# Attention's sums of exponentials: the two key halves added on POOL, one product with ones per head instead of two

## The chip, the cores and the metric

The kernel runs on one core of one Trainium2 chip. The metric is the device time of one execution, in microseconds (us). Engines are named as the profile names them: PE (matrix products), PEld (its weight loads), DVE (VectorE), ACT (ScalarE), POOL (GpSimd) and SP (the queue that issues transfers).

## What is computed

A decoder layer on 16 batches of 256 rows and 512 channels, in float32: self-attention with 16 heads of 32 channels (each of its four linear maps has a low-rank addition), then a decayed scan over a second input, then a feed-forward block with ternary weights and inner size 2048. Each of the three ends in a residual sum and a layer norm. The part that the change touches is the softmax of the attention:

```python
q = _split(lora_linear(x, Wq, bq, Bq, Aq))
k = _split(lora_linear(x, Wk, bk, Bk, Ak))
v = _split(lora_linear(x, Wv, bv, Bv, Av))
scores = jnp.einsum('bhqd,bhkd->bhqk', q, k) * SCALE
attn = jax.nn.softmax(scores, axis=-1)
out = jnp.einsum('bhqk,bhkd->bhqd', attn, v)
...
h = jax.nn.silu(bitlinear158(x, w1, b1))
h = jax.nn.gelu(h, approximate=False)
h = layer_norm(h, ln_g, ln_b)
return bitlinear158(h, w2, b2)
```

## The kernel before, in words

**Work and order.** Every engine has a hand-written program: a loop over j from 0 to 18 whose body works on several batches at once. Batch j is in its attention, batch j-1 in the scan and the first feed-forward product, batch j-2 in the feed-forward layer norm, batch j-3 in the last product. The order within a body is written out by hand on each engine, and every engine works its list in order. Semaphores tie the lists together: `wait(engine, name, b, k)` waits until step k of batch b was counted under that name. For j from 2 to 15 all the attention and all or nearly all of the rest is present; j of 0 and 1 also prepare the weights of the feed-forward block, and j from 16 to 18 have no attention.

**Attention.** The 16 heads are done in four groups of four, c = 0 to 3. The 256 keys are two halves of 128, which lie on the partitions. For each group PE computes the scores with queries on the partitions (`scores`, L1079), and DVE takes the row maxima from them (`maxima`, L769). PE transposes the maxima (`shiftT`, L1088), and ACT stores them (L554). PE then computes the scores again with keys on the partitions and the maxima subtracted (`shifted`, L1103), and ACT takes the exponentials (`probs_of`, L532, two instructions, one per key half) into `probs` (128 partitions; key half x head x 256 queries). PE multiplies them by the values (`weighted`, L1115) and by ones (L1119). The second product sums the exponentials over the keys: per head it is one product per key half, the two accumulated in PSUM, each with 32 columns of ones, so that the sum comes out on the head's 32 partitions of bank 4. `pv_ready` is counted behind the last of them. DVE turns the sums into their inverse and scales the result (`attn_norm`: L785, L787, L789, L794), and POOL splits it into a high and a low part (`attn_split`: L351, L354), which the output product `o` multiplies.

**PE's body**, in order: y(0) (L1189), o(0) (L1056), qk of group 2, scores 1, weighted 0, o(1), shiftT 1, hT(2) and hT(3) (L1182), shifted 1, qk 3, scores 2, weighted 1, y(1), shiftT 2, r(0) and r(1) (L1156), shifted 2, qk 0 of the next batch, scores 3, weighted 2, v(0), shiftT 3, v(1), shifted 3, qk 1 and scores 0 of the next batch, weighted 3, hT(0) and hT(1), xq(0) and xq(1) (L1164, L1165), eight products f (L1172, L1173) with shiftT 0 of the next batch between them, shifted 0 of the next batch. So between the exponentials of a group and its `weighted` stands one `qk` and one `scores`. y, o, r, v, hT, xq and f share PSUM banks 6 and 7, and each waits for the reader of the bank's last content: r(1) for the DVE sum behind y(1) (L917), xq(1) for `hqT_move` (DVE, L910).

**ACT's body** begins with the exponentials of group 0, then `h_var` (L603), `h_norm` (L608). It ends with `silu` of the eight f and two `gelu` (L593).

**POOL's body**: res1 (L406), two `neg_mean` (L433), inverse_std3 (L394 to L399), h_rstd(0) (L440 to L446, which waits for ACT's `h_var`), g_mul(0) (L452), attn_split 0, h_rstd(1), inverse_std1 (L361 to L367), x_lo of the next batch (L343), attn_split 1, g_mul(1), inverse_std3, inverse_std2 (L376 to L386), x_rms (L421 to L428), z_rms, attn_split 2, res2 (L413), z_rms, attn_split 3.

**DVE's body** holds, among others: L917 and L818 (residual sums with L810 and L812), maxima 1, attn_norm 0, z_add(0) (L873, behind g_mul(0)), maxima 2, attn_norm 1, z_max(0) (L878), L917 of y(1), two sums L826 behind r, z_add(1) (L873), maxima 3, attn_norm 2, quantise_x (L847 to L867; waits for ACT's second norm L570, which waits for POOL's inverse_std2), quantise_z(0) (L896 to L903; hT(0) waits for it), maxima 0 of the next batch, hqT_move (L910), attn_norm 3.

Of the kernel before, what the change touches and what calls it, by code (L numbers as in the profile page):

```python
# [7 lines left out]
F32 = mybir.dt.float32  # L8
# [5 lines left out]
ALU = mybir.AluOpType  # L14
AX_X = mybir.AxisListType.X

P = 128
NB = 16
T = 256
NT = T // P  # L20
# [3 lines left out]
HD = D // HEADS  # L24
GH = P // HD
# [25 lines left out]
def decoder_kernel(nc, x, xT, ctxT, W, L, bq, bk, bv, bo, decay, w1T, b1, ln_g, ln_b, w2T, b2, out):  # L51
    b1_scratch = nc.dram_tensor("b1_scratch", (NPART, INNER), BF16, kind="Internal").ap()

    with ExitStack() as ctx:
        def sb(name, shape, dt):
            return ctx.enter_context(nc.sbuf_tensor(name, shape, dt))
# [34 lines left out]
        inverse_T = sb("inverse_T", [P, T // HD], F32)  # L91
        inverse = sb("inverse", [P, T], F32)
        probs = sb("probs", [P, NT, GH, T], F32)
        attn = sb("attn", [P, T], F32)
        attn_hi = sb("attn_hi", [P, KC, T], F32R)
        attn_lo = sb("attn_lo", [P, KC, T], F32R)
# [26 lines left out]
        def sem(name):  # L123
# [44 lines left out]
            (DV, "z_added", 4), (DV, "z_quant", 12),  # L168
            (DV, "ln3", 6), (DV, "hqT_moved", 1),

            (PO, "x_lo", 1), (PO, "attn_split", 8), (PO, "res1", 2), (PO, "res2", 2), (PO, "rstd1", 3),
            (PO, "rstd2", 4), (PO, "rstd3", 6), (PO, "x_rms", 4), (PO, "h_stat", 8), (PO, "g_mul", 2),
            (PO, "z_rms", 4),

# [5 lines left out]
        def wait(eng, name, b, k):  # L180

            if b * per[name] + k > 0:
                eng.wait_ge(S[name], b * per[name] + k)

        def alive(j, lag):

            return 0 <= j - lag < NB
# [34 lines left out]
        def flat(t):  # L222
            return t.rearrange("p a b -> p (a b)")
# [100 lines left out]
        def _(po):  # L324
# [13 lines left out]
            def x_lo(b):  # L338
# [4 lines left out]
                po.tensor_tensor(flat(xT_lo[:, :, :]), flat(xT_in[:, :, :]), flat(xT_hi[:, :, :].bitcast(F32)),  # L343
                                 ALU.subtract).then_inc(S["x_lo"], 1)

            def attn_split(b, c):

                wait(po, "attn_done", b, c + 1)
                if c == 0:
                    wait(po, "o_ready", b - 1, 2)  # L350
                po.tensor_scalar(attn_hi[:, c, :], attn[:, :], 1.0, 0.0, ALU.mult,  # L351
                                 ALU.add).then_inc(S["attn_split"], 1)
                wait(po, "attn_split", b, 2 * c + 1)
                po.tensor_tensor(attn_lo[:, c, :], attn[:, :], attn_hi[:, c, :].bitcast(F32),  # L354
                                 ALU.subtract).then_inc(S["attn_split"], 1)

            def inverse_std1(b):

                r = rstd[:, 0, :, :]
                wait(po, "ln1", b, 6)  # L360
                po.tensor_scalar(r[:, R_VE, :], mean_var[:, 0, :, 1], 1.0, EPS, ALU.mult,  # L361
                                 ALU.add).then_inc(S["rstd1"], 1)
                wait(po, "rstd1", b, 1)
                po.tensor_tensor(r[:, R_USED, :], r[:, R_VE, :], neg_half[:, :], ALU.pow).then_inc(S["rstd1"], 1)
                wait(po, "rstd1", b, 2)
                for q in range(NT):
                    last = po.tensor_scalar(r[:, R_NB, q:q + 1], mean_var[:, 0, q, 0:1], r[:, R_USED, q:q + 1],  # L367
                                            -1.0, ALU.mult, ALU.mult)
                last.then_inc(S["rstd1"], 1)
# [39 lines left out]
            def res2(b):  # L409

                for q in range(NT):
                    wait(po, "x_quant", b, 6 + q)
                    po.tensor_tensor(rows_of(b)[:, q, :], rows_of(b)[:, q, :], b2_tile[:, :],  # L413
                                     ALU.add).then_inc(S["res2"], 1)
# [21 lines left out]
            def h_rstd(b, q):  # L436

                f = fs[:, q, :]
                wait(po, "h_var", b, q + 1)
                po.tensor_scalar(f[:, H_VE:H_VE + 1], f[:, H_VS:H_VS + 1], 1.0 / INNER, EPS, ALU.mult,  # L440
                                 ALU.add).then_inc(S["h_stat"], 1)
                wait(po, "h_stat", b, 3 + 3 * q)
                po.tensor_tensor(f[:, H_RSTD:H_RSTD + 1], f[:, H_VE:H_VE + 1], neg_half[:, 0:1],
                                 ALU.pow).then_inc(S["h_stat"], 1)
                wait(po, "h_stat", b, 4 + 3 * q)
                po.tensor_tensor(f[:, H_NB:H_NB + 1], f[:, H_NMEAN:H_NMEAN + 1], f[:, H_RSTD:H_RSTD + 1],  # L446
                                 ALU.mult).then_inc(S["h_stat"], 1)

            def g_mul(b, q):

                wait(po, "h_normed", b, q + 1)
                po.tensor_tensor(h_of(b, q)[:, :], h_of(b, q)[:, :], g_tile[:, :], ALU.mult).then_inc(S["g_mul"], 1)  # L452
# [22 lines left out]
            def body(j):  # L475
                if alive(j, 1):
                    res1(j - 1)
                if alive(j, 2):
                    neg_mean(j - 2, 0)
                    neg_mean(j - 2, 1)  # L480
                if alive(j, 3):
                    inverse_std3(j - 3, 0)
                if alive(j, 2):
                    h_rstd(j - 2, 0)
                    g_mul(j - 2, 0)
                if alive(j, 0):
                    attn_split(j, 0)
                if alive(j, 2):
                    h_rstd(j - 2, 1)
                if alive(j, 1):  # L490
                    inverse_std1(j - 1)
                if alive(j, -1):
                    x_lo(j + 1)
                if alive(j, 0):
                    attn_split(j, 1)
                if alive(j, 2):
                    g_mul(j - 2, 1)
                if alive(j, 3):
                    inverse_std3(j - 3, 1)
                if alive(j, 1):  # L500
                    inverse_std2(j - 1)
                    x_rms(j - 1)
                if alive(j, 2):
                    z_rms(j - 2, 0)
                if alive(j, 0):
                    attn_split(j, 2)
                if alive(j, 1):
                    res2(j - 1)
                if alive(j, 2):
                    z_rms(j - 2, 1)  # L510
                if alive(j, 0):
                    attn_split(j, 3)
# [522 lines left out]
        def _(pe):  # L1035
# [71 lines left out]
            def weighted(b, c):  # L1107

                wait(pe, "attn_done", b, c)
                wait(pe, "v_stored", b, 2)  # L1110
                wait(pe, "probs_ready", b, 2 * (c + 1))
                for kt in range(NT):
                    for i in range(GH):
                        ch = (GH * c + i) * HD
                        pe.matmul(bank[4][i * HD:(i + 1) * HD, 0:T], v_sb[b % 2][:, kt, ch:ch + HD], probs[:, kt, i, :],  # L1115
                                  start=(kt == 0), stop=(kt == NT - 1))
                for kt in range(NT):
                    for i in range(GH):
                        last = pe.matmul(bank[4][i * HD:(i + 1) * HD, T:2 * T], ones[:, :], probs[:, kt, i, :],  # L1119
                                         start=(kt == 0), stop=(kt == NT - 1))  # L1120
                last.then_inc(S["pv_ready"], 1)


# [221 lines left out]
```

## Time and profile before

| | |
|---|---|
| time of three executions | 1217.88, 1218.5, 1220.4 us; median 1218.5 us |
| profiled execution | time 1219.12 us, span 1216.9 us |
| busy share of the span | PE 88%, PEld 59%, DVE 70%, ACT 68%, POOL 48% |
| mean granted TensorE clock | 0.953 of full speed |
| transfers | 51.79 MB, 43 GB/s on average |

The span is the stretch from the first to the last instruction of the profiled execution; its own time is 2.2 us longer. A busy share is the time in which the engine ran at least one instruction. PE's instructions overlap, and in the rows of the trace an f32 product has two records: a group of eight is `x16`.

### The profile page before, as it was taken

What the parts mean: (1) busy time and instruction counts of PE and PEld (TensorE: products, weight loads), DVE (VectorE), ACT (ScalarE), POOL (GpSimd) and SP (SyncE); (2) the same over time, 40 slices, a digit from 0 to 9 for tenths busy, and PEclk for the clock granted to TensorE, in tenths of its full rate; (3) what the DMA queues carried; (4) which work ended last, traced back from release to release, by engine and by line L of the source; (5) the groups of instructions that cost most, each with busy time, mean ns of one, the idle gap of its engine ahead of it and who ended that gap; (6) DMA issues with size and microseconds to landing.
All of it is one profiled execution on the core that took longest, in us unless ns stands there. A gap on an engine that the chain in (4) does not pass through costs nothing.

```text
span 1216.9 us, 25870 instructions
## 1 busy us (share of the span) xinstructions
PE 1065.3 (88%) x10572; PEld 714.9 (59%) x10572; DVE 851.3 (70%) x1358; ACT 828.5 (68%) x1019; POOL 583.9 (48%) x767
## 2 busy tenths in 40 slices
PE   4977888999999999999999999999999999967253
PEld 3666647575666667575756666675757566643121
DVE  4366938687695968686876959686868769585524
ACT  3555576776778677867767786778677677866472
POOL 2203318273654637282736546372827365463433
PEclk8999889999999999999999999999999999989587
DMA  7522101001010201001010102010010101010000
GB/s 287 190 73 85 53 1 53 1 28 44 13 60 2 71 1 39 33 27 44 28 44 12 60 2 71 2 44 27 28 44 28 44 13 42 1 53 1 18 6 29
DMA packets 17783, 51.79 MB, mean 43 GB/s; under 512 B 2809, under 2 KB 2809, under 8 KB 15874
## 3 DMA queue, kind: packets, MB, share of 16 engines
q1 hardware_dynamic: 16946, 48.31, 11.4%
q8 instruction: 84, 1.38, 0.5%
q10 hardware_dynamic: 720, 1.84, 0.4%
q14 instruction: 33, 0.27, 0.1%
HBM read 41.73 MB, written 8.40 MB: 41 GB/s over the span
## 4 chain that ended last, share of the span: by engine, by line
PE 71%; DVE 11%; ACT 7%; issue 5%; POOL 4%; DMA 1%; SPq 0%; ACTq 0%; POOLq 0%; DVEq 0%
PE bank L1056 29%; PE bank L1172 11%; PE wave L1103 9%; PE bank L1189 5%; PE wave L1079 4%; PE bank L1115 4%; PE bank L1173 3%; PE bank L1119 3%; DVE shift L769 3%; DVE fz L878 2%; POOL h L452 2%; PE bank L1182 2%; ACT hqT L626 2%; ACT h L608 1%; DVE qk_parts L778 1%
## 5 line engine op out<-in xcount | busy, mean ns | idle before, releaser
L769 DVE TENSOR_REDUCE shift<-wave 128x8 f32<-128x2048 f32 x64 | 146.8, 2294 | 102.1 <-PE wave L1079 102.1
L532 ACT ACTIVATE probs<-wave 128x1024 f32<-128x1024 f32 x128 | 124.4, 1024 | 108.9 <-PE wave L1103 108.8
L452 POOL TENSOR_TENSOR h<-h,g_tile 128x2048 f32<-128x2048 f32 x32 | 146.3, 4571 | 42.7 <-ACT h L608 41.2
L1172 PE MATMUL bank<-w,xqT 128*128 128x512 fp8e4 x512 | 135.9, 389 | 12.9 <-ACT invT L579 7.8
L1189 PE MATMUL bank<-w,hqT 128*128 128x512 fp8e4 x512 | 121.0, 391 | 17.3 <-ACT hqT L626 16.4
L587 ACT ACTIVATE h<-bank,qx 128x512 f32<-128x512 f32 x128 | 88.0, 688 | 62.3 <-PE bank L1173 61.0
L433 POOL TENSOR_SCALAR fs<-fs 128x1 f32<-128x1 f32 x32 | 6.2, 192 | 221.1 <-ACT h L593 221.1
L917 DVE SCALAR_TENSOR_TENSOR rows<-bank,fz,rows 128x512 f32<-128x512 f32 x32 | 23.9, 747 | 113.4 <-PE bank L1189 113.4
L1103 PE MATMUL wave<-qk_parts 32*128 32x256 f32 x1536 | 92.0, 337 | 11.2 <-ACT shift_rows L554 11.2
L873 DVE TENSOR_TENSOR h<-h,b_tile 128x2048 f32<-128x2048 f32 x32 | 75.5, 2360 | 36.9 <-POOL h L452 36.9
L1189 PEld LDWEIGHTS bank<-w,hqT 128*128 128x128 bf16 x512 | 48.7, 100 | 84.8 <-ACT hqT L626 18.0
L570 ACT ACTIVATE rows<-rows,rstd 128x512 f32<-128x512 f32 x96 | 74.7, 817 | 31.2 <-POOL rstd L399 11.4
L1056 PE MATMUL bank<-xT_hi,wq_hi 128*128 128x256 f32 x256 | 78.8, 308 | 8.3 <-DVE wk_lo L762 7.2
L1103 PE MATMUL wave<-shift_rows,ones_wide 32*128 32x256 f32 x1024 | 85.6, 397 | 0.0
L1172 PEld LDWEIGHTS bank<-w,xqT 128*128 128x128 bf16 x512 | 41.5, 98 | 70.6 <-issue 22.0
L547 ACT ACTIVATE qk_parts<-bank,bias_qk 128x256 fp32r<-128x256 f32 x128 | 54.0, 479 | 40.5 <-PE bank L1056 40.5
L1103 PEld LDWEIGHTS wave<-qk_parts 32*128 32x128 f32 x1536 | 66.0, 192 | 24.9 <-ACT shift_rows L554 13.7
L351 POOL TENSOR_SCALAR attn_hi<-attn 128x256 fp32r<-128x256 f32 x64 | 26.2, 410 | 109.8 <-DVE attn L794 98.2
L354 POOL TENSOR_TENSOR attn_lo<-attn,attn_hi 128x256 fp32r<-128x256 f32 x64 | 73.8, 1153 | 5.3
L608 ACT ACTIVATE h<-h,fs 128x2048 f32<-128x2048 f32 x32 | 67.4, 2105 | 13.1 <-POOL fs L446 13.1
L1056 PE MATMUL bank<-xT_lo,wq_hi 128*128 128x256 f32 x256 | 73.1, 286 | 0.0
L1056 PE MATMUL bank<-xT_hi,wq_lo 128*128 128x256 f32 x256 | 72.9, 285 | 0.0
(155 smaller groups left out, 3008.2 us busy)
## 6 DMA issues: line engine op xcount, KB each, us to landing
ctx_sb<-ctxT SPq DMA_DIRECT2D x16, 512.0 KB, 3.6
rows<-x SPq DMA_DIRECT2D x16, 512.0 KB, 3.9
out<-rows SPq DMA_DIRECT2D x32, 256.0 KB, 2.1
xT_in<-xT SPq DMA_DIRECT2D x15, 512.0 KB, 5.0
h<-w1T SPq DMA_DIRECT2D x4, 1024.0 KB, 4.9
h<-w2T SPq DMA_DIRECT2D x4, 1024.0 KB, 5.8
h<-Wq SPq DMA_DIRECT2D x1, 1024.0 KB, 6.1
h<-Wk SPq DMA_DIRECT2D x1, 1024.0 KB, 10.2
```

Of the source, the lines that this page charges most:

```text
L354: po.tensor_tensor(attn_lo[:, c, :], attn[:, :], attn_hi[:, c, :].bitcast(F32), ALU.subtract).then_inc(S["attn_split"], 1)
L452: po.tensor_tensor(h_of(b, q)[:, :], h_of(b, q)[:, :], g_tile[:, :], ALU.mult).then_inc(S["g_mul"], 1)
L532: ac.activation(probs[:, kt, :, :], wave[:, :, kt * T:(kt + 1) * T], ACT.Exp, scale=SM_SCALE).then_inc(S["probs_ready"], 1)
L570: ac.activation(rows_of(b)[:, q, :], rows_of(b)[:, q, :], ACT.Identity, scale=r[:, R_USED, :], bias=r[:, R_NB, :]).then_inc(S[f"norm{ln}"], 1)
L587: ac.activation(h_of(b, q)[:, n * FW:(n + 1) * FW], bank_of("f", u), ACT.Silu, scale=qx[:, X_DEQ, q:q + 1]).then_inc(S["silu_done"], 1)
L608: ac.activation(h_of(b, q)[:, :], h_of(b, q)[:, :], ACT.Identity, scale=fs[:, q, H_RSTD:H_RSTD + 1], bias=fs[:, q, H_NB:H_NB + 1]).then_in ...
L769: dv.tensor_reduce(shift[:, :, :, 0].rearrange("p t j -> p j t"), wave[:, :, :].rearrange("p j (t k) -> p j t k", t=NT), axis=AX_X, op=ALU ...
L873: dv.tensor_tensor(h_of(b, q)[:, :], h_of(b, q)[:, :], b_tile[:, :], ALU.add).then_inc(S["z_added"], 1)
L1056: last = pe.matmul(psum, lhsT, rhs, start=(i == 0), stop=(i == len(pairs) - 1))
L1103: last = pe.matmul(bank[head][:, kt * T:(kt + 1) * T], keys, queries, start=(i == 0), stop=(i == 3))
L1172: pe.matmul(p[:, :], xqT[:, q, kc, :], w1[:, kc, n * FW:(n + 1) * FW], start=(kc == 0), stop=False)
L1189: last = pe.matmul(p[:, :], hqT[:, k, :], w2[:, k, :], start=(k == 0), stop=(k == FC - 1))
```

## The change

POOL gets a step `add_halves` for each group: it waits for both key halves' exponentials and for the products of the group before, and adds the two halves of `probs` (128 x 1024 each) into a tile of its own, `half_sum`, of which there is one. In `weighted` PE multiplies that tile by ones, one product per head in place of two. It waits for POOL behind the eight products with the values. In POOL's body the step of group 0 stands between h_rstd(0) and g_mul(0), that of group 1 between inverse_std1 and x_lo, that of group 2 between the second inverse_std3 and inverse_std2, and that of group 3 between res2 and the last z_rms.

```diff
@@ tiles and counts
+        half_sum = sb("half_sum", [P, GH, T], F32)
...
+            (PO, "halves_added", 4),
@@ POOL
+            def add_halves(b, c):
+
+                wait(po, "probs_ready", b, 2 * (c + 1))
+                wait(po, "pv_ready", b, c)
+                po.tensor_tensor(flat(half_sum[:, :, :]), flat(probs[:, 0, :, :]), flat(probs[:, 1, :, :]),
+                                 ALU.add).then_inc(S["halves_added"], 1)
@@ POOL, body(j)
                 if alive(j, 2):
                     h_rstd(j - 2, 0)
+                if alive(j, 0):
+                    add_halves(j, 0)
+                if alive(j, 2):
                     g_mul(j - 2, 0)
...
                 if alive(j, 1):
                     inverse_std1(j - 1)
+                if alive(j, 0):
+                    add_halves(j, 1)
                 if alive(j, -1):
                     x_lo(j + 1)
...
                 if alive(j, 3):
                     inverse_std3(j - 3, 1)
+                if alive(j, 0):
+                    add_halves(j, 2)
                 if alive(j, 1):
                     inverse_std2(j - 1)
                     x_rms(j - 1)
...
                 if alive(j, 1):
                     res2(j - 1)
+                if alive(j, 0):
+                    add_halves(j, 3)
                 if alive(j, 2):
                     z_rms(j - 2, 1)
@@ PE, weighted(b, c)
-                for kt in range(NT):
-                    for i in range(GH):
-                        last = pe.matmul(bank[4][i * HD:(i + 1) * HD, T:2 * T], ones[:, :], probs[:, kt, i, :],
-                                         start=(kt == 0), stop=(kt == NT - 1))
+                wait(pe, "halves_added", b, c + 1)
+                for i in range(GH):
+                    last = pe.matmul(bank[4][i * HD:(i + 1) * HD, T:2 * T], ones[:, :], half_sum[:, i, :],
+                                     start=True, stop=True)
                 last.then_inc(S["pv_ready"], 1)
```

The order of POOL's instructions from h_rstd(0) of one body to x_lo, in the kernel before (`fs` holds the feed-forward statistics, `h` its rows):

```order
L440 TENSOR_SCALAR fs<-fs 128x1 [waits h_var]
L443 TENSOR_TENSOR fs<-fs,neg_half 128x1 [waits h_stat]
L446 TENSOR_TENSOR fs<-fs 128x1 [waits h_stat]
L452 TENSOR_TENSOR h<-h,g_tile 128x2048 [waits h_normed]
L351 TENSOR_SCALAR attn_hi<-attn 128x256 [waits o_ready,attn_done]
L354 TENSOR_TENSOR attn_lo<-attn,attn_hi 128x256 [waits attn_split]
...
L367 TENSOR_SCALAR rstd<-mean_var,rstd 128x1 [waits rstd1]
L367 TENSOR_SCALAR rstd<-mean_var,rstd 128x1
L343 TENSOR_TENSOR xT_lo<-xT_in,xT_hi 128x1024 [waits v_ready,qk_ready,x_hi]
```

And the same stretch in the changed kernel, whose lines stand eight further down the file:

```order
L448 TENSOR_SCALAR fs<-fs 128x1 [waits h_var]
L451 TENSOR_TENSOR fs<-fs,neg_half 128x1 [waits h_stat]
L454 TENSOR_TENSOR fs<-fs 128x1 [waits h_stat]
L351 TENSOR_TENSOR half_sum<-probs 128x1024 [waits pv_ready,probs_ready]
L460 TENSOR_TENSOR h<-h,g_tile 128x2048 [waits h_normed]
L359 TENSOR_SCALAR attn_hi<-attn 128x256 [waits o_ready,attn_done]
L362 TENSOR_TENSOR attn_lo<-attn,attn_hi 128x256 [waits attn_split]
...
L375 TENSOR_SCALAR rstd<-mean_var,rstd 128x1 [waits rstd1]
L375 TENSOR_SCALAR rstd<-mean_var,rstd 128x1
L351 TENSOR_TENSOR half_sum<-probs 128x1024 [waits pv_ready,probs_ready]
L344 TENSOR_TENSOR xT_lo<-xT_in,xT_hi 128x1024 [waits v_ready,qk_ready,x_hi]
```

The sum of group 0 now stands behind h_rstd(0) and its wait for ACT, and ahead of g_mul(0); that of group 1 stands behind g_mul(0) and everything up to inverse_std1, ahead of x_lo.

PE's `weighted` of a group in the changed kernel (`bank` is bank 4), where eight products `bank<-probs,ones` without a wait of their own stood before:

```order
L1132 MATMUL bank<-probs,v_sb 32x256 [waits probs_ready,v_stored]
L1132 MATMUL bank<-probs,v_sb 32x256 x7
L1136 MATMUL bank<-half_sum,ones 32x256 [waits halves_added]
L1136 MATMUL bank<-half_sum,ones 32x256 x3
```

Four products are gone, and the first of the remaining four waits for POOL.

## Rows read from the trace of the kernel before

**Rows 1.** The page's chain that ended last: shares of the span by engine.
```profile
PE 71%; DVE 11%; ACT 7%; issue 5%; POOL 4%; DMA 1%; SPq 0%; ACTq 0%; POOLq 0%; DVEq 0%
```
**Rows 2.** Windows: one body: length; busy us (count) of PE, PEld, DVE, ACT, POOL; PEclk; DMA.
```profile
503.80:570.70 66.90, 63.92 (x659) 43.47 (x658) 50.59 (x82) 49.37 (x63) 35.44 (x47) 1.00 0.11 33
```
**Rows 3.** Groups by line and form: line, engine, tiles, shapes, count | busy, mean ns | idle before.
```profile
L1119 PE MATMUL bank<-probs,ones 128*32 128x256 f32 x1024 | 68.2, 384 | 0.0
...
L343 POOL TENSOR_TENSOR xT_lo<-xT_in,xT_hi 128x1024 fp32r<-128x1024 f32 x16 | 37.9, 2369 | 18.2 <-ACT xT_hi L540 18.2
...
L452 POOL TENSOR_TENSOR h<-h,g_tile 128x2048 f32<-128x2048 f32 x32 | 146.3, 4571 | 42.7 <-ACT h L608 41.2
...
L361 POOL TENSOR_SCALAR rstd<-mean_var 128x2 f32<-128x2 f32 x16 | 3.1, 193 | 1.6 <-DVE mean_var L812 0.4
...
L859 DVE TENSOR_SCALAR qx<-qx,w_mean 128x2 f32<-128x2 f32 x16 | 19.9, 1246 | 0.0
```
**Rows 4.** PE in order of time, that body: start, length, instruction [idle before it].
```profile
514.78 1.05 PE L1119 MATMUL bank<-probs,ones 128*32 128x256 f32 x16
...
526.67 1.05 PE L1119 MATMUL bank<-probs,ones 128*32 128x256 f32 x16
...
533.42 0.66 PE L1156 MATMUL bank<-ident,ctx_sb 128*128 128x128 f32 x4 [1.49 <-DVE rows L917]
...
540.60 1.05 PE L1119 MATMUL bank<-probs,ones 128*32 128x256 f32 x16
...
554.12 1.05 PE L1119 MATMUL bank<-probs,ones 128*32 128x256 f32 x16
555.10 1.07 PE L1182 MATMUL bank<-ident_bf,h 128*128 128x128 bf16 x16
...
557.47 0.40 PE L1164 MATMUL bank<-ident_bf,x_round 128*128 128x128 bf16 x4
```
**Rows 5.** ACT in order of time, the same body.
```profile
513.28 0.20 ACT L603 ACTIVATION_READ_ACCUMULATOR junk<-h,fs 128x1 f32 x1
...
535.93 1.94 ACT L532 ACTIVATE probs<-wave 128x1024 f32<-128x1024 f32 x2 [3.32 <-PE wave L1103]
...
541.78 1.53 ACT L570 ACTIVATE rows<-rows,rstd 128x512 f32<-128x512 f32 x2
...
549.44 1.94 ACT L532 ACTIVATE probs<-wave 128x1024 f32<-128x1024 f32 x2 [0.46 <-PE wave L1103]
```
**Rows 6.** POOL in order of time, the same body.
```profile
514.46 0.19 POOL L446 TENSOR_TENSOR fs<-fs 128x1 f32<-128x1 f32 x1
...
521.91 2.66 POOL L354 TENSOR_TENSOR attn_lo<-attn,attn_hi 128x256 fp32r<-128x256 f32 x1
...
526.92 0.51 POOL L367 TENSOR_SCALAR rstd<-mean_var,rstd 128x1 f32<-128x1 f32 x2
...
537.48 2.15 POOL L376 TENSOR_SCALAR rstd<-mean_var 128x2 f32<-128x2 f32 x1 [0.47 <-DVE mean_var L812]
```
**Rows 7.** DVE in order of time, the same body.
```profile
521.50 2.48 DVE L873 TENSOR_TENSOR h<-h,b_tile 128x2048 f32<-128x2048 f32 x1 [1.00 <-POOL h L452]
...
528.11 0.44 DVE L785 STREAM_TRANSPOSE sums_T<-bank 128x256 f32<-128x256 f32 x1
...
532.62 0.74 DVE L917 SCALAR_TENSOR_TENSOR rows<-bank,fz,rows 128x512 f32<-128x512 f32 x1
...
537.31 2.26 DVE L873 TENSOR_TENSOR h<-h,b_tile 128x2048 f32<-128x2048 f32 x1
...
544.36 1.21 DVE L847 TENSOR_REDUCE qx<-rows 128x2 f32<-128x1024 f32 x1
...
551.12 0.16 DVE L899 TENSOR_TENSOR fz<-fz 128x1 f32<-128x1 f32 x1
...
551.56 1.29 DVE L903 TENSOR_SCALAR h<-h,fz 128x2048 f32<-128x2048 f32 x1
...
556.27 0.69 DVE L910 TENSOR_SCALAR hqT<-bank 128x1024 bf16<-128x1024 int16 x1 [0.63 <-PE bank L1182]
```

More of the change, by code:

```diff
@@ L169, in decoder_kernel @@
             (DV, "ln3", 6), (DV, "hqT_moved", 1),
-            (PO, "x_lo", 1), (PO, "attn_split", 8), (PO, "res1", 2), (PO, "res2", 2), (PO, "rstd1", 3),
+            (PO, "x_lo", 1), (PO, "halves_added", 4), (PO, "attn_split", 8), (PO, "res1", 2), (PO, "res2", 2), (PO, "rstd1", 3),
             (PO, "rstd2", 4), (PO, "rstd3", 6), (PO, "x_rms", 4), (PO, "h_stat", 8), (PO, "g_mul", 2),
```

## The prediction

> **What bounds the kernel now.** I read the chain of waits first: 71% of the span is PE's work [rows 1]. Then one body in the middle, j = 7: of 66.9 us PE is busy 63.9 at the full granted clock, POOL 35.4 [rows 2]. The bodies of j = 2 to 14 repeat this to about 0.1 us, so I walk through one, at the absolute times of the trace, and multiply. The longest idle time of PE in it is the 1.49 us ahead of r(1), where it waits for DVE's L917 [rows 4]. PE has next to no slack: a microsecond saved counts nearly in full, and so does one of new waiting.
>
> **What PE saves.** The products with ones of a group take 0.98 us from the first to the instruction behind them (554.12 to 555.10) [rows 4], and this holds for each of the 64 groups, whose 1024 records are one group of lines [rows 3]. Half of the products gone is 0.49 us a group, if half the work takes half the time: 1.96 us a body.
>
> **What the add costs POOL.** The trace has no such add. The nearest rows are x_lo, same engine, type of operation and element count, 2.37 us, and half of g_mul, 4.57/2 = 2.29 us [rows 3]. I take 2.3 us. POOL goes from 35.4 to 44.6 us a body: not the bound. What matters is when each add ends and when PE wants it. I reckon 0.6 us from the add's end to the next work of PE (0.05 for the wait, then four products alone: 1.05 - 0.49 us, the group's length less half of its stretch) [rows 4].
>
> **Group 0: a wait of 2.2 us.** PE wants the sum at 514.78 [rows 4]. The add stands behind h_rstd(0). That waits for ACT's h_var, which ends at 513.48 [rows 5], and L446 ends at 514.65 [rows 6]. The add runs from 514.7 to 517.0. PE's next work starts at 517.6 instead of 515.76: **+1.85 us**, the saved half counted. The path to 514.65 runs over f, silu, gelu, the exponentials and h_var, and nothing in it becomes shorter. g_mul(0) starts 0.1 us later.
>
> **Group 1: little more.** POOL then does g_mul(0) to 521.6 and attn_split. z_add(0) on DVE (L873) begins where the split's second half does. Before, L354 took 2.66 us and ended 0.6 us behind L873 [rows 6, 7]; L376, of the form for which L361 takes 0.19 us, took 2.15 us beside the other L873 and ended with it [rows 3, 6, 7]. So an L873 (both inputs in SBUF) stops POOL for its own 2.3 us. Now the split gets in first, z_add runs 522.8 to 525.1, and it is h_rstd(1) that is stopped. inverse_std1 ends at 527.85 (before 527.43) [rows 6], and the add runs 527.9 to 530.2. PE wants it at 526.67 + 1.85 = 528.5: it waits 1.7 us. The sums are ready at 530.8, and attn_norm starts then instead of at 528.11 [rows 7]: DVE is 2.7 us late, with it L917, and with that r(1) on PE. PE, 3.1 us late, gives up most of its old wait there [rows 4]. Both stand at **+2.7 us**. If POOL escaped the stop, DVE would be late by its maxima alone, +1.85.
>
> **Group 2: stopped by z_add(1).** Both chains start at L917: exponentials that ended at 537.87 [rows 5], z_add(1) at 537.31 to 539.57 [rows 7]. z_add is 0.56 us ahead and stays so. At +2.7 it runs 540.0 to 542.3. The add is free to start at 540.6. No row shows two large operations meeting here; between no wait at all and a wait to the end of z_add I take the latter, as L376 showed it. The add runs 542.3 to 544.6, PE wants it at 543.3, and goes on at 545.2 instead of 541.58: **+3.6 us** (without the stop +2.7 - 0.49 = +2.2). The Trainium skill, SBUF — State Buffer, "Who interferes with whom", says that a VectorE instruction with two SBUF inputs and a GpSimd instruction that reads SBUF exclude each other, and that the one issued first keeps the port pair for its whole length. By that rule the group gives +3.6; if the two shared the port it would give +2.2. The small operations of the trace agree with the rule; whether a large add does is not shown.
>
> **Behind group 2.** inverse_std2 now stands behind that add. ACT's second norm began 2.15 us behind L376's end [rows 5, 6]. With the 2.3 us of the tiny operations and nothing to hide them it begins at about 547.05 (+5.3), and quantise_x on DVE at 548.65, not 544.36 (+4.3) [rows 7]. L899 is then due at 555.4. **Group 3's** exponentials end at 551.38 + 3.6 = 555.0 [rows 5], and POOL, long through with res2, adds from 555.0 to 557.3. PE wants it at 557.7: no wait, -0.49. But L899 has two SBUF inputs. L859, a tiny operation beside POOL's res2, takes 1.25 us where L899 takes 0.16 [rows 3, 7]: POOL stops DVE too. So L899 waits to 557.3, L903 ends at 559.1, and hT(0), due on PE at 555.10 + 3.1 = 558.2, starts at 559.15. The next maxima follow, then hqT_move at 561.5 (before 556.27) [rows 7], and xq(1), which needs its bank, starts at 562.25 instead of 557.47 [rows 4]. Through ACT's silu the products f end up at about **+4.5 us**. Without this last effect: +3.1.
>
> **Moved steps and other queues.** x_lo now ends at 532.5; qk of the next batch, which reads it, stands behind shifted 2 and begins at 538.5, so it is hidden. g_mul(1) ends at 538.3, before z_add(1) is due at 540.0: 1.7 us in hand. res2 and attn_split 3 have more. Were that cover gone, each microsecond would go into z_add(1), and so into the add of group 2. SP's and ACT's lists issue no transfer more or later than their bodies. The new wait on PE holds up the output products or y behind it, which is what the sums above count. One `half_sum` tile does no harm: the wait for the group before is long met.
>
> **The sum.** Thirteen bodies (2 to 14) at +4.5 = +58.5 us. Body 15 lacks the next batch's work, and has the same order on POOL: about +4. Bodies 0 and 1 have an idle POOL and can only gain, between 0 and 8 x 0.49 = 3.9 us: -2. The tail has no attention: 0. Together +60.5 us. The profiled execution goes from a span of 1216.9 to 1277.4 us, with the 2.2 us around it 1279.6. Its own time before, 1219.12, is 0.6 above the median of the three executions, 1218.5, so the median becomes **1279 us**, 5.0% more.
>
> **The rivals.**
> 1. *The stops are smaller* (chance 0.28). Group 0's wait stays, since it hangs on ACT alone, but the port costs less, or quantise_z slips in ahead of the add. With the stop of group 2 and no later effect a body loses 1.85 + 0.85 + 0.9 - 0.49 = 3.1 us; with group 0's alone, and groups 2 and 3 saving 0.49 each, 0.9 us (group 1's saving is lost, as r(1) waits for DVE). Times 14, less the 2 us of bodies 0 and 1: 1229 to 1260. For it: the margins in group 3 are 0.4 us. Against: both L354 and L376 are stopped in full.
> 2. *The adds are hidden* (0.05), the other side. The mechanism is PE's saving with the add of group 0 early enough. It decides at 514.78: POOL would have to start by 512.4, 2.3 us earlier than L446's end lets it. Then three groups save 0.49 us and group 1's is lost, 1.47 x 14 + 2 = 23 us: 1196. For it: exponentials of groups 1 to 3 end 2.7 us before the sums are wanted. Against: the order of POOL's list.
> 3. *Four products take as long as eight* (0.08). They lie on four column groups and overlap; if the four that are left cost the 0.98 us of the eight, the saving of 1.96 us a body is none: 14 x 1.96 = 27 us more, 1306. Against: the 16 records of a group are evenly spread over the 0.98 us.
>
> **How the numbers follow.** The forecast has 0.57, the three rivals 0.28, 0.05 and 0.08, and 0.02 is left for no change. A measurement of this kernel can tell about 0.2%, 2.4 us, from no change. Faster by more than that: 0.05; within it: 0.03; slower: 0.92, from the forecast, rivals 1 and 3 and a small rest. The forecast's own range is 1260 to 1292, from the bounds of the last effect (1.4 us a body) and of the add (2.29 to 2.37 us). With most of rival 1 below and part of rival 3 above, the range is 1238 to 1296.
>
> **What would show it right or wrong.** In the changed profile: POOL's add x64 at about 2.3 us, those of group 2 longer, about 4 us, with the stop in them. PE idle ahead of the products with ones, released by POOL: 2.2 us a body in group 0, about 1.7 in group 1, about 1.3 in group 2, none in group 3. The products with ones half as long in all. A body of 71.4 us in place of 66.9. Second norm and quantise_x late, L899 waiting beside the add. Wrong would be: no wait in group 0; an add that isn't stopped beside L873; a body shorter than 67 us.

## The result, and the profile after

The changed kernel takes 1330.22 us (median of four executions, 1324.56 to 1335.95), against 1218.46 us before. The ratio is 1.091, 95% interval 1.086 to 1.097. It is slower, as forecast, but by 112 us and not by 60, and the time lies 34 us above the range. The profiled execution took 1324.56 us, with a span of 1321.4 us.

The page of the changed kernel: busy time by engine, granted PE clock in 40 slices, and the chain that ended last.

```profile
PE 1091.7 (83%) x10060; PEld 698.2 (53%) x10060; DVE 897.3 (68%) x1358; ACT 827.6 (63%) x1019; POOL 732.9 (55%) x831
...
PEclk9998799999999999989989898999989898977677
...
PE 26%; POOL 25%; DVE 19%; ACT 17%; issue 11%; DMA 1%; SPq 0%; POOLq 0%; ACTq 0%; DVEq 0%
```

PE's share of the chain was 71% [rows 1]; now POOL has a quarter, and DVE and ACT have more than before. PE is busy *longer* than before, 1091.7 against 1065.3 us, with 512 records fewer. That is the surprise of this page, and the clock row is the hint: it has 8s in the second half, where the row of the kernel before has 9s.

Two bodies of the changed kernel, windows with the columns of [rows 2]. They start at the first y of the body:

```profile
457.80:529.20 71.40, 62.91 (x627) 42.05 (x627) 53.43 (x82) 49.35 (x63) 44.94 (x51) 1.00 0.09 31
529.20:604.40 75.20, 67.08 (x628) 42.80 (x628) 53.42 (x82) 49.39 (x63) 44.94 (x51) 0.93 0.09 29
```

Both issue the same work, and DVE, ACT and POOL are busy alike. The first is 71.4 us long, as predicted. In the second PE's granted clock averages 0.93, PE is busy 4.2 us longer, and the body is 3.8 us longer. The bodies of j = 3 to 6 are of the first kind, 71.37 or 71.38 us each, those of j = 7 to 14 of the second, 75.1 to 75.2.

PE in order of time in the body of j = 7. The numbers answer to [rows 4]:

```profile
542.39 0.64 PE L1136 MATMUL bank<-half_sum,ones 128*32 128x256 f32 x8 [2.04 <-POOL half_sum L351]
...
555.23 0.64 PE L1136 MATMUL bank<-half_sum,ones 128*32 128x256 f32 x8 [1.18 <-POOL half_sum L351]
...
561.25 0.66 PE L1173 MATMUL bank<-ident,ctx_sb 128*128 128x128 f32 x4 [1.17 <-DVE rows L934]
...
569.68 0.64 PE L1136 MATMUL bank<-half_sum,ones 128*32 128x256 f32 x8 [1.06 <-POOL half_sum L351]
...
582.70 0.61 PE L1136 MATMUL bank<-half_sum,ones 128*32 128x256 f32 x8
...
584.84 1.05 PE L1199 MATMUL bank<-ident_bf,h 128*128 128x128 bf16 x16 [1.52 <-DVE h L920]
586.71 0.61 PE L1181 MATMUL bank<-ident_bf,x_round 128*128 128x128 bf16 x4 [0.82 <-ACT hqT L643]
...
588.53 1.87 PE L1189 MATMUL bank<-w,xqT 128*128 128x512 fp8e4 x4 [0.18 <-ACT invT L596]
```

The waits for POOL are where they were forecast: 2.04, 1.18 and 1.06 us in groups 0 to 2, none in group 3. So is the wait of hT(0) for DVE, 1.52 us (the walk had 0.95). The last row is the one that was not forecast. Each of the eight products f is four matrix products of 128x512 on L1189 and one on L1190; the four of the first f take 1.87 us. The same place in the body of j = 4:

```profile
370.70 1.05 PE L1199 MATMUL bank<-ident_bf,h 128*128 128x128 bf16 x16 [1.52 <-DVE h L920]
372.58 0.40 PE L1181 MATMUL bank<-ident_bf,x_round 128*128 128x128 bf16 x4 [0.82 <-ACT hqT L643]
...
374.14 1.02 PE L1189 MATMUL bank<-w,xqT 128*128 128x512 fp8e4 x4 [0.18 <-ACT invT L596]
```

There the lead-up is the same, the same 1.52 and 0.82 us of waits, but the clock holds. In the body of j = 7 the transposes behind the second wait already take 0.61 us instead of 0.40: the clock falls ahead of the products f.

POOL, ACT and DVE of the body of j = 7, with the stops:

```profile
548.17 2.11 POOL L448 TENSOR_SCALAR fs<-fs 128x1 f32<-128x1 f32 x1
...
552.81 2.37 POOL L351 TENSOR_TENSOR half_sum<-probs 128x1024 f32<-128x1024 f32 x1
...
565.79 3.84 POOL L351 TENSOR_TENSOR half_sum<-probs 128x1024 f32<-128x1024 f32 x1 [1.13 <-ACT probs L549]
...
580.13 2.39 POOL L351 TENSOR_TENSOR half_sum<-probs 128x1024 f32<-128x1024 f32 x1 [0.76 <-ACT probs L549]
```
```profile
572.05 1.52 ACT L587 ACTIVATE rows<-rows,rstd 128x512 f32<-128x512 f32 x2 [2.58 <-POOL rstd L394]
```
```profile
565.14 2.26 DVE L890 TENSOR_TENSOR h<-h,b_tile 128x2048 f32<-128x2048 f32 x1
...
573.61 1.22 DVE L864 TENSOR_REDUCE qx<-rows 128x2 f32<-128x1024 f32 x1 [0.81 <-ACT rows L587]
...
580.25 2.29 DVE L913 TENSOR_TENSOR fz<-fz 128x1 f32<-128x1 f32 x1
```

h_rstd(1)'s first operation is stopped for 1.9 us by z_add(0), which runs from 547.6 to 550.2; the add of group 2 takes 3.84 us, since z_add(1) (L890) has the port until 567.4; the second norm and quantise_x are late; and a 128x1 operation of quantise_z takes 2.29 us beside the add of group 3 (580.13 to 582.52), where its like alone takes 0.16 [rows 7]. The stop reaches L913, the first operation with two SBUF inputs, and not L899's counterpart three further on: the same wait, met a little earlier.

**Where the 104.4 us of span come from.** Counted from the first y of body 3: before it +7.6 us (start at 243.69, before 236.09); bodies 3 to 14 at +4.44 us, +53.3 (66.93 became 71.37); in bodies 7 to 14 another 3.7 each, +29.9; body 15 +11.9 (74.94 for 63.04); the tail +1.7.

### The profile page after: what moved, and what is told of

The parts are those of the page before. It is cut to its first block, busy times and chain, and to the rows that moved or that the text cites. A ratio compares the mean times of both kernels' runs of the same rounds, so it can differ in the third digit from the quotient of the medians.

```text
span 1321.4 us, 24973 instructions
## 1 busy us (share of the span) xinstructions
PE 1091.7 (83%) x10060; PEld 698.2 (53%) x10060; DVE 897.3 (68%) x1358; ACT 827.6 (63%) x1019; POOL 732.9 (55%) x831
## 4 chain that ended last, share of the span: by engine, by line
PE 26%; POOL 25%; DVE 19%; ACT 17%; issue 11%; DMA 1%; SPq 0%; POOLq 0%; ACTq 0%; DVEq 0%
PE bank L1189 12%; POOL half_sum L351 9%; POOL h L460 5%; PE bank L1190 3%; PE wave L1120 3%; POOL fs L448 3%; ACT h L610 3%; ACT junk L620 2%; PE bank L1073 2%; DVE fz L895 2%; ACT probs L549 2%; DVE fz L913 2%; ACT rows L587 2%; ACT L610 2%; POOL fs L451 1%
## 5 line engine op out<-in xcount | busy, mean ns | idle before, releaser
L351 POOL TENSOR_TENSOR half_sum<-probs 128x1024 f32<-128x1024 f32 x64 | 171.9, 2686 | 69.2 <-ACT probs L549 57.4
L549 ACT ACTIVATE probs<-wave 128x1024 f32<-128x1024 f32 x128 | 124.3, 1024 | 105.2 <-PE wave L1120 105.1
L1189 PE MATMUL bank<-w,xqT 128*128 128x512 fp8e4 x512 | 169.6, 465 | 8.2 <-ACT w L651 5.0
L890 DVE TENSOR_TENSOR h<-h,b_tile 128x2048 f32<-128x2048 f32 x32 | 79.2, 2474 | 22.4 <-POOL h L460 22.4
L1136 PE MATMUL bank<-half_sum,ones 128*32 128x256 f32 x512 | 41.4, 396 | 63.4 <-POOL half_sum L351 63.2
L1189 PEld LDWEIGHTS bank<-w,xqT 128*128 128x128 bf16 x512 | 46.6, 109 | 86.1 <-issue 54.9
L1199 PE MATMUL bank<-ident_bf,h 128*128 128x128 bf16 x512 | 38.2, 225 | 60.3 <-DVE h L920 57.6
L643 ACT ACTIVATE hqT<-bank,neg_int 128x1024 bf16<-128x1024 int16 x48 | 51.7, 1115 | 44.5 <-PE bank L1199 44.5
```

The lines of the kernel that those rows point to most:

```text
L351: po.tensor_tensor(flat(half_sum[:, :, :]), flat(probs[:, 0, :, :]), flat(probs[:, 1, :, :]), ALU.add).then_inc(S["halves_added"], 1)
L549: ac.activation(probs[:, kt, :, :], wave[:, :, kt * T:(kt + 1) * T], ACT.Exp, scale=SM_SCALE).then_inc(S["probs_ready"], 1)
L890: dv.tensor_tensor(h_of(b, q)[:, :], h_of(b, q)[:, :], b_tile[:, :], ALU.add).then_inc(S["z_added"], 1)
L1189: pe.matmul(p[:, :], xqT[:, q, kc, :], w1[:, kc, n * FW:(n + 1) * FW], start=(kc == 0), stop=False)
```

## The experiments

Each was timed beside the kernel before on the same chip. A body's length is the distance of its first y from the next. In most of them the question was one of two: does PE's clock account for the part that the prediction lacks, and do the steps of the walk account for the rest?

**1. Work in PE's gap.** Six products that nobody reads, into the bank that hT(0) overwrites, where PE waits 1.5 us for DVE.

```diff
             def hT(j, n):
                 q = n // 2
+                if n == 0:
+                    free = take(j, "h", 0, "v_stored", 0, 1)
+                    for _ in range(6):
+                        pe.matmul(free[:, :], ident_bf[:, :], w1[:, 0, 0:FW], start=True, stop=True)
                 p = take(j, "h", n, "z_quant", j - 2 - q, 6 * (q + 1))[:, :].bitcast(BF16)
```

> The changed kernel, with six idle products (128x128 by 128x512 into the bank that hT(0) overwrites, about 0.22 us each) on PE ahead of hT(0), where PE waits 1.5 us for DVE in each body. Theory clock: about 35 to 45 us of the loss are PE's clock granted at the 1.2 GHz level in the first f products, brought on by PE's idle stretches ahead of them. With work in one of these the body goes from 75.1 back to 71.4 us, PEclk of a body to 1.00, and the kernel from about 1330 to 1285-1295. Rival load: the clock falls for a reason that filling this gap does not touch, or the stretched f products have another cause: the body stays at 75.1 us, 1330 or a little more.

Measured: 1288.5 us (1286.54 to 1289.99), 1.056 times the kernel before. **More work on PE makes the changed kernel 42 us faster.** The bodies are 71.36 to 71.38 us long, every second or third 72.2 to 72.3. Two of them, windows as above:

```profile
383.20:526.90 143.70, 130.18 (x1265) 86.04 (x1265) 106.38 (x164) 98.68 (x125) 90.01 (x102) 0.99 0.09 31
```

The theory of the clock holds: only PE's idle time was filled, and the clock of the f products came back. The two profiled spans differ by 36.7 us (1321.4 less 1284.7): 27 in bodies 7 to 14, the rest at the ends of the program (3.2 ahead of body 3, 5.3 in body 15, 1.8 behind it, less 0.9 in bodies 3 to 6). The medians differ by more, 42, because the profiled execution of the changed kernel was its fastest. A remainder stays, the longer bodies. In them the clock falls at another place, right behind PE's wait of 2.04 us in group 0, where the products with ones take 1.01 us instead of 0.64:

```profile
396.42 1.01 PE L1136 MATMUL bank<-half_sum,ones 128*32 128x256 f32 x8 [2.04 <-POOL half_sum L351]
```

**2. The same six products in the kernel before**, as a control.

> The kernel before with the same six idle products ahead of hT(0), as a control of the run that filled the gap. PE does not wait there before, so they cost their own time: 6 x 0.216 = 1.3 us a body, 16 bodies, about 1239, and PEclk stays 1.00 in the middle. Rival: idle products by themselves speed something up (a change of phase): below 1225.

Measured: 1234.49 us, ratio 1.012 (1.011 to 1.014). A body is 68.2 us, 1.29 more than 66.93, the products' own time:

```profile
506.10:574.30 68.20, 65.23 (x666) 44.05 (x666) 50.59 (x82) 49.35 (x63) 35.35 (x47) 1.00 0.10 32
```

In these bodies, whose clock is full with and without the products, they only cost. The twelve bodies 3 to 14 make 15.5 us, about what the medians differ by, 15.3. The forecast of 1239 was 5 us too much: it counted 16 bodies at the full price. Ahead of body 3, where the clock of both kernels falls again and again, this one is 2.9 us faster (233.16 for 236.09), so some of what experiment 1 gained at the ends of the program may not be the change's own loss.

**3. Idle time without POOL.** The kernel before, with two unused maxima on DVE ahead of quantise_z(0).

```diff
                 if alive(j, 2):
+                    for k in range(2):
+                        dv.tensor_reduce(fz[:, 0, 8 + k:9 + k], g_tile[:, :], axis=AX_X, op=ALU.max,
+                                         apply_absolute_value=True)
                     quantise_z(j - 2, 0)
```

> The kernel before, without any add on POOL, with two unused maxima of 128x2048 (2.3 us each, 4.6 us) on DVE ahead of quantise_z(0), whose result hT(0) waits for. DVE had about 2.2 us in hand, so hT(0) starts 2.4 us late and xq(1) about 3 us: a body of 69.9 us and, with the clock kept, about 1258-1265. Theory clock: idle time of PE at this place is what lowers the clock in the f products, whoever causes it: the body is then 2 to 4 us longer still (72 to 74) in some or all bodies, PEclk of a body 0.93 to 0.97, 1285-1310. Rival: it takes the adds on POOL to bring the clock down: 1258-1265, PEclk 1.00.

Measured: 1297.1 us (1290.3 to 1298.99), ratio 1.062. Bodies are 71.1 to 73.2 us long. One of them:

```profile
381.40:452.70 71.30, 66.45 (x659) 43.92 (x658) 54.78 (x84) 49.42 (x63) 35.38 (x47) 0.95 0.10 31
```

and PE in it, ahead of the products f and in them:

```profile
434.91 1.05 PE L1185 MATMUL bank<-ident_bf,h 128*128 128x128 bf16 x16 [2.21 <-DVE h L903]
436.79 0.61 PE L1167 MATMUL bank<-ident_bf,x_round 128*128 128x128 bf16 x4 [0.82 <-ACT hqT L626]
...
438.61 1.86 PE L1175 MATMUL bank<-w,xqT 128*128 128x512 fp8e4 x4 [0.18 <-ACT invT L579]
```

Every body is above the 69.9 us of the kept clock. hT(0) waits 2.2 us and the four matrix products of the first f take 1.86 us: the clock falls at the same place with no add in the program. So it is PE's idle time that matters, not what POOL does.

**4. What the four products are worth.** No adds, no wait; `half_sum` is filled with ones once.

```diff
@@ POOL: the four add_halves left out
+            po.memset(flat(half_sum[:, :, :]), 1.0).then_inc(u_pool, 1)
@@ PE, weighted
-                wait(pe, "halves_added", b, c + 1)
```

> The changed kernel without the adds and without PE's wait for them; half_sum is set to ones once, so the divisor is wrong and no sum of the exponentials is computed. What the four products less are worth to PE alone. Theory: 0.49 us in three of four groups, none in group 1 where r(1) waits for DVE: 1.47 us a body, about 1196. Rival: four products on four column groups take as long as eight: 1218.

Measured: 1210.64 us (1206.58 to 1213.46), ratio 0.992 (0.990 to 0.995). Most bodies are 65.65 us:

```profile
430.80:496.40 65.60, 62.10 (x627) 42.29 (x626) 50.47 (x82) 49.23 (x63) 35.33 (x47) 1.00 0.09 33
```

The saving is 1.28 us a body, near the 1.47 worked out from the rows, so four products on four column groups do take about half the time of eight. But four of the twelve bodies 3 to 14 are 67.15 us long. In each of them the clock falls behind r(1), where PE's wait for DVE has grown from 1.49 to 1.92 us because PE arrives earlier:

```profile
392.89 0.66 PE L1164 MATMUL bank<-ident,ctx_sb 128*128 128x128 f32 x4 [1.92 <-DVE rows L926]
...
394.88 1.08 PE L1112 MATMUL wave<-shift_rows,ones_wide 32*128 32x256 f32 x8
```

The like of the last row takes 0.60 us in a body of 65.65. Body 15 loses 4.2 us as well (67.23 for 63.04, at a mean clock of 0.82 for 0.92). So the total saves only 8 us, and neither the theory (23) nor the rival (none) had it. Even with the sum for nothing the change would have brought 0.8%. An add on another engine had little to win here.

**5. What POOL's occupation costs.** The kernel before, with the four adds at the places of the change, and nobody reading them.

```diff
@@ PE, weighted: as in the kernel before (eight products from probs, no wait for POOL)
@@ POOL, add_halves
-                wait(po, "pv_ready", b, c)
@@ ACT, probs_of
                 wait(ac, "pv_ready", b, c)
+                wait(ac, "halves_added", b, c)
```

> The kernel before (eight products with ones from probs), with the four adds on POOL at the places of the change; nobody reads half_sum, and ACT's next exponentials wait for the add. What POOL's occupation alone costs. Theory: the add of group 2 is stopped by z_add(1) and holds up inverse_std2 and the second norm, the add of group 3 stops L899, xq(1) is about 1 us late: body 67.9, about 1232 without the clock, and up to 1285 if PE's clock falls in the f products as in the changed kernel. Rival: POOL's work is hidden, 1218.

Measured: 1310.75 us (1308.87 to 1317.45), ratio 1.076. My figure for the clock kept, 67.9 us a body, was wrong: bodies are 72.7 and 74.0 us long, in turn, and the time lies above the 1285 us too. ACT's new wait for the adds costs nothing: those of groups 0 to 2 end 5.1 to 6.7 us ahead of the exponentials that wait for them. POOL, DVE and PE in one of them:

```profile
568.43 2.29 POOL L401 TENSOR_SCALAR rstd<-mean_var 128x1 f32<-128x1 f32 x1
...
571.68 2.40 POOL L350 TENSOR_TENSOR half_sum<-probs 128x1024 f32<-128x1024 f32 x1
```
```profile
578.07 1.22 DVE L864 TENSOR_REDUCE qx<-rows 128x2 f32<-128x1024 f32 x1 [2.89 <-ACT rows L587]
...
583.92 2.31 DVE L884 TENSOR_TENSOR qx<-qx,inv_parts 128x2 f32<-128x2 f32 x1
```
```profile
578.84 0.63 PE L1120 MATMUL wave<-qk_parts 32*128 32x256 f32 x12 [0.81 <-ACT shift_rows L571]
...
589.34 1.12 PE L1199 MATMUL bank<-ident_bf,h 128*128 128x128 bf16 x16 [2.85 <-DVE h L920]
```

My walk had left the second inverse_std3 in front of z_add(1). With g_mul(1) late, z_add(1) (568.4 to 570.7) starts first and stops it for 2.1 us; only then come the add of group 2 and inverse_std2. The second norm is late, ACT's next store makes PE wait 0.81 us, quantise_x waits 2.89 us, an operation of it is stopped for 2.1 us, and hT(0) waits 2.85 us. So adds whose sums nobody reads cost 92 us of the 112 that the changed kernel loses, the lowered clock included (0.95 and 0.93 in the two kinds of body). With the clock kept a body would be about 70.2 us, an estimate: 72.7 less the 2.5 us by which bodies of the same mean clock are longer in experiment 7. That is 1.2 us under the 71.4 of the full change, though PE there waits 4.3 us a body for the sums of groups 0 to 2. Most of those waits is no price on top: they make z_add(1) late as well (35.9 us into the body, here 34.1), so that it no longer stops inverse_std3.

**6 and 7. Two groups at a time.** In the first, groups 0 and 1 have the add and the four products; in the second, groups 2 and 3. The other groups are as before.

```diff
@@ PE, weighted (GROUPS is (0, 1) or (2, 3); POOL has add_halves of these groups only)
+                if c in GROUPS:
+                    wait(pe, "halves_added", b, GROUPS.index(c) + 1)
...
+                else:
+                    for kt in range(NT):
...
```

> Adds and four products for groups 0 and 1 only; groups 2 and 3 as in the kernel before. By the prediction's steps these two cost +2.7 us a body, to which the later ones add nothing: body 69.6 us, 1255 with the clock kept, up to 1300 with it lowered. Rival (from the run with the unused adds, where a body was late through inverse_std3 and inverse_std2 on POOL though PE waited for no sum): most of the loss is the POOL time of these two adds ahead of g_mul(1), and PE's waits for the sums are not what costs; then DVE's quantise_x starts 2 us or more late in this run too, with no add between the two inverse_std steps.

Measured: 1259.0 us, ratio 1.033 (1.030 to 1.035). A body of 69.4 us with the clock kept, and 70.3 in between:

```profile
511.70:581.10 69.40, 63.53 (x643) 42.78 (x642) 50.84 (x82) 49.37 (x63) 39.94 (x49) 1.00 0.09 32
```

quantise_x starts 10.95 us behind r(1), as before (10.94); the rival falls. PE waits for the sums 2.04 and 1.18 us, as in the full change. In the bodies of 70.3 us the clock falls behind the wait of group 0.

> Adds and four products for groups 2 and 3 only; groups 0 and 1 as before. Walk with the rows of before: z_add(1) stops the add of group 2 (a record of about 4 us), PE goes on 0.9 us late; inverse_std2 ends 2.4 us late, quantise_x starts 1.5 us late; the add of group 3 stops L899's like for up to 2 us; hT(0) 1.3 us late, xq(1) 2 us. Body 68.9 us, 1244 with the clock kept, up to 1290 with it lowered. Rival: if the two adds cost nothing, 1210 (0.49 us saved twice).

Measured: 1270.55 us, ratio 1.043 (1.040 to 1.046). 68.93 us a body with the clock kept, others 70.0 to 71.6:

```profile
379.70:448.70 69.00, 63.40 (x644) 42.80 (x644) 53.17 (x82) 49.40 (x63) 40.40 (x49) 1.00 0.09 32
517.60:589.00 71.40, 66.20 (x643) 43.34 (x642) 53.17 (x82) 49.29 (x63) 40.29 (x49) 0.95 0.09 31
```

Both clean bodies are the walk's to 0.2 us. They add up: 66.93 + 2.45 + 2.00 = 71.38, the body of the full change. Fourteen bodies at +2.45 and +2.00 would make 1253 and 1246 us. The rest goes with a lowered clock and is larger in the second (24 us for 6): there it falls between hT and the products f, behind waits of 1.52 and 0.82 us.

**8. The add of group 0 first.** It goes ahead of h_rstd(0) on POOL.

```diff
+                if alive(j, 0):
+                    add_halves(j, 0)
                 if alive(j, 2):
                     h_rstd(j - 2, 0)
-                if alive(j, 0):
-                    add_halves(j, 0)
-                if alive(j, 2):
                     g_mul(j - 2, 0)
```

> The changed kernel with the add of group 0 ahead of h_rstd(0) on POOL. Theory queue: POOL's list from g_mul(0) on sets when the add of group 1 ends, so the 2.0 us wait of group 0 goes, and that of group 1 grows from 1.2 to about 3.5; a body gains about 0.4 us, 6 us in all (1324). Rival additive: each wait counts by itself, a body gains 2.0 + us and the kernel about 30 us (1300). The clock may hide either by some 30 us: compare the places within a body.

Measured: 1327.73 us, ratio 1.089 (1.087 to 1.091), the time of the change within its interval. PE in one body has no wait left in group 0, and this one in group 1:

```profile
492.60 1.08 PE L1135 MATMUL bank<-half_sum,ones 128*32 128x256 f32 x8 [3.72 <-POOL half_sum L351]
```

Additive waits are refuted. The 2.0 us come back in the next group, since POOL's list from g_mul(0) on does not start earlier. It even starts 0.45 us later (13.55 for 13.10 us into the body), as h_rstd(0) now stands behind the add, so the small gain that the theory had is not there either. One wait of 3.7 us in place of two is also no kinder to the clock: it falls in every body, and the bodies are 72.2 to 77.6 us long.

**9. The sums of group 3 behind hT.** POOL adds after quantise_z(0), and PE does these four products behind hT(0) and hT(1).

```diff
@@ POOL, add_halves
+                if c == 3 and b >= 2:
+                    wait(po, "z_quant", b - 2, 6)
@@ PE, body(j)
                 if alive(j, 2):
                     hT(j, 0)
                     hT(j, 1)
+                if alive(j, 0):
+                    sums(j, 3)
```

> The changed kernel, but in group 3 the add on POOL waits until quantise_z(0) is through, and PE does the products with ones of group 3 behind hT(0) and hT(1). Theory: the add no longer stops DVE's small operations (2.1 us), hT(0) starts at once, the sums fill PE's wait for hT's store, and the clock stays up: a body of about 70 us, PEclk 1.00, about 1270. Rival: the clock falls anyway: about 73.7 us a body, 1310.

Measured: 1289.63 us, ratio 1.058. The shortest body is 70.2 us at full clock, as the theory says, and hT(0) no longer waits. But others are 71.1, 72.7 and 74.0 to 74.2 us long with a lower clock, so the outcome lies between the two expectations. The edit does two things, and together they are worth 1.2 us a body: the stop is gone, and the four products are out of hT's way. PE now waits 1.1 to 1.3 us for the add there. The clock is helped, not cured: in ten of the twelve bodies 3 to 14 it falls behind the 2.04 us of group 0, and in four of these also in the products f.

**10. A version that beats both.** No adds at all. At r(1) PE waits for L917, 1.49 us in the kernel before [rows 4] and 1.17 us in the changed one.

```diff
@@ DVE, body(j)
                 if alive(j, 0):
                     maxima(j, 2)
-                    attn_norm(j, 1)
...
                 if alive(j, 3):
                     layernorm3_sum(j - 3, 1)
+                if alive(j, 0):
+                    attn_norm(j, 1)
@@ POOL, body(j)
-                if alive(j, 0):
-                    attn_split(j, 1)
                 if alive(j, 2):
                     g_mul(j - 2, 1)
+                if alive(j, 0):
+                    attn_split(j, 1)
```

> The kernel before, no adds; on DVE attn_norm of group 1 stands behind the residual sum of y(1) (L917), and on POOL g_mul(1) ahead of attn_split of group 1. All runs so far show r(1) on PE waiting about 1.2 to 1.5 us a body for L917, which stands behind attn_norm 1. Theory: L917 comes 1.6 us earlier, PE's 1.5 us wait there goes, nothing else is later, a body of 65.5 us and about 1199. Rival: the 1.5 us turn up again at hT(0) or xq(1), because quantise_x on DVE does not start earlier (second norm, inverse_std2 behind z_add(1)): body 66.9, 1218; or the longer idle time there lowers the clock, 1225 and more.

The expectation's "all runs so far" is not exact: the wait was 1.92 us in experiment 4 and 0.19 us in experiment 8. Measured: 1202.93 us (1199.84 to 1206.38, five executions), ratio 0.987 (0.985 to 0.989). A body is 65.63 us, the clock full; the wait at r(1) is 0.19 us:

```profile
499.20:564.80 65.60, 63.92 (x660) 43.44 (x660) 50.72 (x82) 49.22 (x63) 35.13 (x47) 1.00 0.10 33
```
```profile
527.46 0.65 PE L1157 MATMUL bank<-ident,ctx_sb 128*128 128x128 f32 x4 [0.19 <-DVE rows L917]
```

It computes all that the kernel before computes, and is 1.3% faster: the same queues that made the change slow, read for the wait that is already there.

## Why the prediction was right and wrong

**The body: right.** 71.4 us forecast, 71.37 measured in bodies 3 to 6. That the two meet so closely is in part luck: groups 0 and 1 cost less than forecast, groups 2 and 3 more. *Group 0:* a wait of 2.2 us, measured 2.04; it hangs on ACT's h_var, as said. *Group 1:* 1.7 us, measured 1.18; h_rstd(1) was stopped by z_add(0) as said, but the add began 0.5 us earlier than in the walk (552.81, less the 25.38 us by which this body starts later, is 527.43, not 527.9). Experiment 6 gives +2.45 for +2.7. *Group 2:* a stop by z_add(1), record of about 4 us, measured 3.84. The Trainium skill (SBUF — State Buffer, "Who interferes with whom") says that the one issued first keeps the port pair for the whole instruction; the trace now agrees for a large operation too: 3.84 us is the 1.6 us that z_add(1) still runs and 2.2 us of add. *Behind group 2:* norm and quantise_x late, an operation of quantise_z stopped beside the add of group 3, hT(0) late. Experiment 7 has groups 2 and 3 together at +2.00, where the terms from +2.7 to +4.5 are +1.8.

**The saving on PE:** 0.49 us a group by the rows and, with group 1's lost at r(1) as rival 2 had it, 1.47 us a body; 1.28 measured (experiment 4).

**The step that failed** is the first paragraph's use of [rows 2], "PE is busy 63.9 at the full granted clock", and with it the sum "Thirteen bodies (2 to 14) at +4.5": it took every product of PE at the length that it has at the full clock. The clock was granted at the full level in the middle of the kernel before, and I carried it over without asking what new idle time does to it. In the changed kernel PE has some 1.5 us of new wait right ahead of hT(0), followed by short work and the old wait of 0.8 us; in bodies 7 to 14 the clock then goes to the lower level, 1.2 GHz, and the first f's four matrix products take 1.87 in place of 1.02 us. These bodies come out 29.9 us longer in all than at the full clock. Body 2, a term of +4.5 less 2 for the bodies ahead of it, came to +7.6, and body 15, a term of +4, to +11.9; both have a lower clock in the windows than before. Body 15 is not the clock alone: PE waits in it 3.20 us for ACT ahead of `shifted` of group 3 and 2.24 us at hT(0), before 1.36 and 0.32, and how its loss divides is not shown. In all 44 us are missing in the sum, and experiment 1 gives 37 back in the span by busying PE at one place. The Trainium skill has a page that would have made this a rival, TensorE: Matmul & The Clock Gate, "Part 1": the clock is at the lower rate unless activity holds it up. The trace agrees with that much. [Rows 2] alone could not show it, since the clock never falls in that body. But the table of the kernel before has a mean granted clock of 0.953, so the clock fell elsewhere in it.

**What this means for the range.** None of the rivals held the case; the upper end came from the products' length, not from the clock. Nor does the 1292 follow from its own bounds: four adds of 2.37 instead of 2.3 us are 0.3 us a body, 4 us in all. A term "clock lowered in the f products" was at hand. The eight f take about 10.5 us in a body at the full clock (body 4), so all of them at half speed would have been as much again, some 147 us in 14 bodies, an estimate and an upper bound; 3.7 us came of it, in eight bodies.

**Still open.** Up to the place where the clock falls, PE's waits in bodies 3 to 6 are those of bodies 7 to 14 to 0.01 us, and the clock holds in them. The executions differ in the same way: 1324.56, 1328.32, 1332.13 and 1335.95 us go with a mean clock of 0.920, 0.908, 0.905 and 0.900. What decides between a body that falls and one that does not was not tried.

## What to carry to other kernels

Before moving work from a full engine to an idle one, read three things: where in the idle engine's list the work would stand and what that position waits for, which two-input operations of DVE it meets at the port, and who waits for everything behind it. Here adds that nobody read cost 92 us, and the products that they were to replace were worth 8. And in a kernel that lives on PE, price new idle time twice: once as time, and once as clock, above all ahead of a long run of products.

## What the runs showed of the hardware beyond what was expected

The granted clock falls after short waits that are broken by small work: 1.52 us, 1.05 us of transposes, 0.82 us (changed kernel, bodies 7 to 14). Four products of 128x512 then take 1.87 us instead of 1.02. It also falls behind a single wait with PE at work on both sides: 2.04 us (experiments 1, 6 and 9) and 1.92 us (experiment 4), in some bodies and not in others. Behind the 1.49 us at r(1) in the kernel before it does not fall in any of the bodies 3 to 14. Useless products of 1.3 us in the first wait make the kernel 42 us faster, and cost 1.29 us a body where PE does not idle.

A 128x1 operation on POOL can take 2.1 us and one on DVE 2.3 us, when the other engine is in a large operation that reads SBUF. Which of the small ones is hit depends on tenths of a microsecond, and it need not be the one that the walk picked.
